# Splitting the 64-wide attention's scores into high and low fp32r parts, with its weights streamed in on every pass

## The reference

```python
def _L1_xattn_ref(x, latents, mask, ...):    # x = ctx_1024, latents = _layernorm(x_main)
    xn, ln = layernorm(x, ...), layernorm(latents, ...)
    q = ln @ Wq                                       # [256, 8 heads x 64]
    k, v = split(concatenate([xn, ln], axis=1) @ Wkv) # 512 keys: 256 of the context, 256 of the tokens
    sim = einsum('bhid,bhjd->bhij', q * scale, k) * scale
    sim = where(full_mask, sim, max_neg)              # only context keys can be masked
    attn = softmax(sim)
    out = einsum('bhij,bhjd->bhid', attn, v)
    return layernorm(out @ Wo, ...)
```

## Time and profile before

| | us |
|---|---|
| median of three runs | 5651.34 |
| profiled execution, its own time | 5660.27 |
| span of the profiled execution | 5658.5 |
| PE busy / share of the span | 4888.0 / 86% |
| DVE busy | 2758.3 / 49% |
| ACT busy | 1853.5 / 33% |
| mean granted TensorE clock, share of full speed | 0.921 |

### The profile page before, as it was taken

The page is one execution under the profiler, slowest core; times in us unless marked ns, Lnnn a source line. Parts: engine busy times, 40 slices in busy tenths (PEclk is TensorE's granted clock), DMA queues, the critical chain, the costliest instruction groups (busy, mean ns, idle before and its releaser), DMA issues.

```text
span 5658.5 us, 74258 instructions
## 1 busy us (share of the span) xinstructions
PE 4888.0 (86%) x29184; PEld 3477.8 (61%) x29184; DVE 2758.3 (49%) x7346; ACT 1853.5 (33%) x3068; POOL 95.5 (2%) x180
## 2 busy tenths in 40 slices
PE   2898878989799897998979988899888998889988
PEld 1556765567656685565855658556585565855657
DVE  3535455354553545436454454544545445454454
ACT  2422324233242333423233242332424324242242
POOL 0000000000000000000000000000000000000000
PEclk9898989999899898998989989799897998989989
DMA  6000210002000020000200002000020000200002
GB/s 273 1 1 22 88 50 1 1 22 112 26 1 1 22 112 26 1 9 21 105 26 1 15 23 97 26 1 14 31 90 26 1 22 23 90 26 1 22 23 94
DMA packets 47155, 218.95 MB, mean 39 GB/s; under 512 B 4544, under 2 KB 16832, under 8 KB 27072
## 3 DMA queue, kind: packets, MB, share of 16 engines
q1 hardware_dynamic: 46784, 213.90, 10.2%
HBM read 192.91 MB, written 20.97 MB: 38 GB/s over the span
## 4 chain that ended last, share of the span: by engine, by line
PE 70%; DVE 19%; ACT 5%; issue 3%; DMA 2%; SPq 0%; POOL 0%; DVEq 0%; ACTq 0%
PE w L418 16%; PE w L428 10%; DVE mx L1023 6%; PE o L559 6%; PE w L675 6%; PE w L517 5%; PE w L667 4%; PE w L408 4%; PE w L531 4%; PE o L552 4%; PE w L484 2%; ACT oth L786 2%; PE w L534 1%; PE w L571 1%; PE w L467 1%
## 5 line engine op out<-in xcount | busy, mean ns | idle before, releaser
L824 ACT ACTIVATE pt<-w 128x1024 f32<-128x1024 f32 x640 | 653.8, 1024 | 768.6 <-PE w L534 440.4
L1023 DVE TENSOR_REDUCE mx<-w 128x4 f32<-128x1024 f32 x512 | 593.7, 1218 | 171.9 <-PE w L467 155.1
L559 PE MATMUL o<-pt,va 128*32 128x256 f32 x4096 | 559.5, 410 | 18.7 <-ACT pt L824 18.7
L786 ACT ACTIVATE oth<-w,res 128x256 f32<-128x256 f32 x656 | 264.1, 475 | 731.0 <-PE w L667 599.8
L1259 DVE TENSOR_REDUCE mx<-w 128x2 f32<-128x1024 f32 x128 | 156.9, 1226 | 527.0 <-PE w L519 527.0
L418 PE MATMUL w<-xnT,res 128*128 128x256 f32 x1408 | 375.3, 418 | 33.8 <-ACT xnT L778 24.5
L667 PE MATMUL w<-qsp,ksp 128*128 128x256 f32 x2048 | 350.3, 289 | 0.0
L418 PEld LDWEIGHTS w<-xnT,res 128*128 128x128 f32 x1408 | 281.3, 208 | 98.8 <-issue 47.6
L559 PEld LDWEIGHTS o<-pt,va 128*32 128x32 f32 x4096 | 207.9, 114 | 194.1 <-issue 67.8
L467 PE MATMUL w<-ksp,qsp 32*128 32x256 f32 (+1 forms) x2048 | 260.9, 401 | 73.5 <-DVE mx L1023 41.5
L418 PE MATMUL w<-xnT,stream 128*128 128x256 f32 x1280 | 311.8, 391 | 0.0
(11 more groups left out here) (235 smaller groups left out, 7506.6 us busy)
## 6 DMA issues: line engine op xcount, KB each, us to landing
stream_lo<-split SPq DMA_DIRECT2D x64, 1024.0 KB, 4.8
ksp<-split SPq DMA_DIRECT2D x64, 1024.0 KB, 6.9
stream<-in_moe_dram SPq DMA_DIRECT2D x80, 384.0 KB, 3.6
va<-in_moe_dram SPq DMA_DIRECT2D x8, 1024.0 KB, 10.3
split<-ksp SPq DMA_DIRECT2D x8, 1024.0 KB, 5.6
split<-qsp SPq DMA_DIRECT2D x8, 1024.0 KB, 8.0
res<-in_resident_dram SPq DMA_DIRECT2D x1, 8157.5 KB, 22.1
cx<-in_ctx_dram SPq DMA_DIRECT2D x16, 256.0 KB, 3.6
```

Source lines behind the costliest of these rows:

```text
L559: mm = pe.matmul(o[g:g + 32, 0:T], by_heads(plan, s)[:, kt, plan.v_of(h), :], pt[:, n % EXPS, a * 512 + kt * T:a * 512 + (kt + 1) * T], st ...
L786: h = act.activation(dst[:, c, :], w[:, c * T:(c + 1) * T], func, bias=bias[:, c:c + 1], **more)
L824: act.activation(pt[:, n % EXPS, :], w[:, :], ACT.Exp, scale=scale).then_inc(S["s_P"], 1)
L1023: dve.tensor_reduce(mx[s][:, :, 2 * u:2 * u + 2].rearrange("p t a -> p a t"), w[:, :].rearrange("p (a t k) -> p a t k", a=2, t=TT), AX_X, ...
```

## The change

- The score matmuls of `l1` are done in fp32r. `k1` now has one chunk per head: 64 partitions hold the rounded keys (high), the other 64 hold what the rounding lost (low). Per head there are two matmuls instead of one fp32 one: the rounded query, laid out twice over both halves (in `qsp`), against the stacked keys, and the query's low part, with zeros in the other half, against the same keys. The product of both low parts is left out.
- Low parts of even heads lie over `xnT` and `xt`, which are idle then; those of odd heads have a buffer `qodd` of their own, zeroed once before the loop. DVE zeroes half of the shared ones in each `l1.q`.
- `l1.q` costs ACT four copies of 64 partitions and DVE two memsets and three subtractions; `l1.kc` and `l1.kl` cost ACT two copies and DVE two subtractions. A new semaphore tells DVE that ACT's copy is done, and the PSUM buffer is free only after DVE's subtraction.
- The mask's two operands become 128 rows high, `maskb` and `first_row`, with zeros below row 0.
- To make room, `l1_wkv`, `l1_wq`, `l1_wo` (4096 columns, 2 MB) and `f3_w1` (2048 columns, 1 MB) leave the resident block. In each pass the first three are loaded into `stream`, between the context and the tokens in SP's list, and `f3_w1` after the seventh `f2` expert. The first five `f1` experts wait until the `l1` weights under them have been used, in both slots.
- `ORDER` is unchanged.

```diff
-        ksp, k1 = shared("ksp", [P, 8, T], F32R, "k1", [P, 4, L1_KEYS])
+        k1, ksp = shared("k1", [P, L1_HEADS, L1_KEYS], F32R, "ksp", [P, 8, T], F32R)
+        qodd = per_slot("qodd", [P, 4, T], F32R)
...
+        def q_low(s, h):
+            return (qodd[s][:, h // 2, :] if h % 2 else q_even[s][h // 4][:, h // 2 % 2, :])
...
                 if what in ("cT", "xT"):
+                    pe.wait_ge(S["s_l1w"], 16)
...
-                        pe.matmul(w[:, tt * 512:(tt + 1) * 512], qz[s][:, u, tt * P:(tt + 1) * P],
-                                  k1[s][:, u // 2, :], start=True, stop=False)
-                        mm = pe.matmul(w[:, tt * 512:tt * 512 + T], ones_row[:, 0:P], maskb[s][:, :], start=False, stop=True)
+                        for n, q in enumerate((qsp[s][:, u, :], q_low(s, u))):
+                            pe.matmul(w[:, tt * 512:(tt + 1) * 512], q[:, tt * P:(tt + 1) * P], k1[s][:, u, :],
+                                      start=(n == 0), stop=False)
+                        mm = pe.matmul(w[:, tt * 512:tt * 512 + T], first_row[:, 0:P], maskb[s][:, :], start=False, stop=True)
...
-                        pe.matmul(o, k1[s][:, u // 2, kt * P:(kt + 1) * P], qz[s][:, u, :], start=True, stop=False)
+                        for n, q in enumerate((qsp[s][:, u, :], q_low(s, u))):
+                            pe.matmul(o, k1[s][:, u, kt * P:(kt + 1) * P], q, start=(n == 0), stop=False)
...
                     elif step == "l1.q":
                         w = full(act, step, s)
-                        for half in range(2):
-                            h = act.activation(qz[s][:, half::2, :], chunks_of(w, 4), ACT.Copy, scale=W_["half"][:, half:half + 1])
-                        h.then_inc(S["s_qz"], 1)
+                        for odd in range(2):
+                            for rows in range(2):
+                                h = act.activation(qsp[s][64 * rows:64 * rows + 64, odd::2, :],
+                                                   chunks_of(w, 4)[64 * odd:64 * odd + 64], ACT.Copy)
+                        h.then_inc(S["s_qhi"], 1)
                     elif step in ("l1.kc", "l1.kl"):
-                        evac(k1[s][:, :, o:o + T], chunks_of(full(act, step, s), 4), "s_k1")
+                        for odd in range(2):
+                            r = slice(64 * odd, 64 * odd + 64)
+                            h = act.activation(k1[s][r, odd::2, o:o + T], chunks_of(w, 4)[r], ACT.Copy)
+                        h.then_inc(S["s_k1hi"], 1)
...
+                    elif step == "l1.q":                      # DVE
+                        for part in q_even[s]:
+                            dve.memset(part[64:128].bitcast(F32), 0.0)
+                        dve.wait_ge(*after("s_qhi", step, s))
+                        for n, part in enumerate(q_even[s]):
+                            dve.tensor_tensor(part[0:64], w[0:64, 2 * n:2 * n + 2], qsp[s][0:64, 4 * n:4 * n + 4:2, :].bitcast(F32), ALU.subtract)
+                        h = dve.tensor_tensor(qodd[s][64:128], w[64:128], qsp[s][64:128, 1::2, :].bitcast(F32), ALU.subtract)
+                        h.then_inc(S["s_qz"], 1)
+                    elif step in ("l1.kc", "l1.kl"):          # DVE
+                        dve.wait_ge(*after("s_k1hi", step, s))
+                        for odd in range(2):
+                            r, other = slice(64 * odd, 64 * odd + 64), slice(64 - 64 * odd, 128 - 64 * odd)
+                            h = dve.tensor_tensor(k1[s][other, odd::2, o:o + T], w[r], k1[s][r, odd::2, o:o + T].bitcast(F32), ALU.subtract)
+                        h.then_inc(S["s_k1"], 1)
...
+                sp.dma_start(stream[:, :], resident_in[:, RESIDENT_COLS:RESIDENT_COLS + LATE_COLS]).then_inc(S["s_l1w"], 16)
                 sp.wait_ge(s_out, 16 * SLOTS)
...
+                        for name, steps in (("l1_wkv", ("l1.kc", "l1.vc", "l1.kl", "l1.vl")), ("l1_wq", ("l1.q",)), ("l1_wo", ("l1.out",))):
+                            if n * MOE1_COLS < late[name][1] and (n + 1) * MOE1_COLS > late[name][0]:
+                                for step in steps:
+                                    used(step, 0)
...
+                for e in range(MOE2 - RING2, MOE2):
+                    if e % RING2 == 0:
+                        used("f2.down", e)
+                sp.dma_start(stream[:, 0:2048], resident_in[:, RESIDENT_COLS + LATE_COLS:]).then_inc(S["s_f3w"], 16)
```

More of the change, by code:

```diff
@@ L55 @@
     ("l3_wq", 512), ("l3_wk", 512), ("l3_wv", 512), ("l3_bq", 2), ("l3_bk", 2), ("l3_bv", 256),
[1 row of a table removed]
[1 row of a table added]
 ]
+LATE = [("l1_wkv", 2048), ("l1_wq", 1024), ("l1_wo", 1024)]
+LAST = [("f3_w1", 2048)]
 RESIDENT_COLS = sum(n for _, n in RESIDENT)
+LATE_COLS = sum(n for _, n in LATE)
+RESIDENT = RESIDENT + LATE + LAST
 STAGE = [("sel8q", 256), ("sel8k", 256), ("sel16q", 256), ("sel16k", 256), ("sel1", 1024), ("f3_w2", 2048)]
@@ L238, in build @@
         at, W_ = 0, {}
-        for name, n in RESIDENT:
+        for name, n in RESIDENT[:-len(LATE + LAST)]:
             W_[name] = res[:, at:at + n]
@@ L262, in build @@
         stream_lo = over("stream_lo", [P, STREAM_COLS])
+        W_["f3_w1"] = stream[:, 0:2048]
+        late, at = {}, 0
+        for name, n in LATE:
+            W_[name] = stream[:, at:at + n]
+            late[name] = (at, at + n)
+            at += n
         pt = sb("pt", [P, EXPS, 1024])
@@ L1172, in _ @@
             dve.memset(onesf[:, :], 1.0)
-            dve.memset(ones_row[:, :], 1.0)
+            dve.memset(first_row[:, :], 0.0)
+            for s in range(SLOTS):
+                dve.memset(maskb[s][:, :], 0.0)
+                dve.memset(qodd[s][:, :, :].bitcast(F32), 0.0)
             dve.memset(mp[:, :, :], 0.0)
```

34 lines of the change are left out of this document (21 added, 13 removed), and 4 rows, old and new, of tables (RESIDENT, SIGNALS).

## The result

| | before | after |
|---|---|---|
| median, us | 5651.34 | 5613.78 (5 runs, 5613.03 to 5617.67) |
| ratio, 95% interval | | 0.9943 [0.9925, 0.9962] |
| span of the profiled execution, us | 5658.5 | 5611.2 |
| mean granted TensorE clock | 0.921 | 0.901 |
| mean length of passes 2 to 8, us | 694.9 | 690.9 |

The account below looks back on a forecast made before the run. PE was taken to bound the `l1` attention. Per pass 39.6 us removed, 22.8 plus 6 for the clock added, net 10.8; with the start 91 in eight passes, giving 5560 us, range 5465 to 5660 (forecast's own 5500 to 5620).

Parts of the forecast that it names:

- PE work removed: `l1` scores: `l1.exp` 18.2 us and `l1.max` 21.4 us less on PE, together 39.6 us a pass.
- Rival 1: Half-height copies and subtractions take half the time and the clock stays up: 13.9 us a pass more, 5449; chance 0.10.
- Start of a pass: Tokens and mask land 5.3 us later behind the 2 MB load; 1.1 us of slack, so 4.2 lost a pass.
- `l1.kc`, slot 0: Slot 1's `l0.norm` waits in DVE's queue behind the key subtractions; PE's transposes come 4.2 us later.
- `l1.kc`, slot 1: Turn, add and `l1.ln` of slot 0 wait behind DVE's subtractions; transposes of `l1.xT` start 5.0 us later.
- `l1.q`: Slot 0: slot 1's turn waits behind DVE's query subtractions; PE's transposes of its result start 6.0 us later.
- Clock: Lower granted clock behind three new holes, about 2 us each: 6 us a pass, bounds 0 and 14.
- In-stage waits: Second slot's `l1.q` and `l1.kl`, and `l1.max` meeting DVE's reductions and turns: 3.4 us a pass, between 0 and 8.
- Once: Before the first pass: smaller resident block, less DVE's memsets, saves 5 us once (0 to 8.3).
- Rival 2: Mask matmul keeps 0.31 us instead of 0.12: 12.2 us a pass, time 5657, no measurable change; chance 0.15.
- Rival 3: Clock stays low through the `l1` scores after the holes: slower, 5744 with half of them affected; chance 0.07.
- Rival 4: Freed PE time goes to waits in `l1`, 15 us a pass instead of 3.4: 5653; chance 0.08.

Follow-up runs that it names:

- fill: Changed kernel with five extra fp32 matmuls, results unused, on PE ahead of the waits of `l0.xT:0` and `f0.cT:1:1`: 5574.81 us, ratio 0.9856.
- mask_row: Changed kernel with the mask's two operands one row high again: 5695.29 us, ratio 1.0073 to the kernel before.
- before_mask: Kernel before the change with only the mask's operands made 128 rows high: 5516.12 us, ratio 0.9777.

## Why the prediction was right in direction and wrong in size

- **PE work removed, 39.6 us: right, in part by luck.** From the table of tiles it is 16 x (2 x 0.674 + 2 x 0.390 + 2 x 0.182) = 39.9. Inside it two errors cancel: the mask's part is 16.1 us, not 12.2, and the split's is 23.8, not 27.4. The fp32r matmuls of 512 columns start 0.31 and 0.24 us apart from what follows, near the value taken and far from the bound of 0.53.
- **Durations of ACT and DVE: right.** A copy of 64 partitions takes 4.11 / 4 = 1.03 us, a subtraction 1.23. Rival 1 (half height, half time) is refuted.
- **Start of a pass, 4.2 us: mis-sized.** I took tokens and mask 5.3 us late. They came 6.9 us late in the fourth pass (17.20 for 10.34), 6.0 by the median of seven. Of the 1.1 us of slack little was there: PE starts `l0.xT` 5.6 us later. It then runs at half clock, which brings 9.9, of which 7.5 are left at the end of `l0`; the sum had 6.2 with its share of the clock. Moving the load is worth 6.6 a pass.
- **`l1.kc`, slot 0, 4.2 us: right at its place, and short behind it.** The transposes of `l0.oT` stand 4.4 us later against the end of `l1.kc`, but up to the end of `l0.out` it is 6.1, since `l0.out` runs at half clock (3.78 us for 1.97). I had given this one of the four holes no share of the clock.
- **`l1.kc`, slot 1, 5.0 us**: 5.3 in the trace, for the 7.0 with its share of the clock, and mostly through another wait, 3.39 us for the PSUM buffer; the late `l1.ln` holds `l1.xT` up for 1.25. I had cost the late release of a buffer nowhere.
- **`l1.q`, 6.0 us: right**, 6.00 in the trace. With the slower steps behind it the place costs 9.0 (18.1 to 27.0), beside the 8 that the sum had for it with its share of the clock.
- **Clock, 6 us: short, inside its bounds.** From 0.921 and 0.901 the time at the low level is 0.079 x 5658 / 0.5 = 894 us before and 1111 after, 27 a pass more; in passes 2 to 8 it is 112 and 143 a pass, 32 more. At 0.24 to 0.38 us for each, as between passes of one kernel, that is an estimated 8 to 12 us; it lies partly in the terms above. `fill` shows 6 us a pass for two places alone.
- **In-stage waits, 3.4 us**: 39.9 less the 34.8 measured is 5.1.
- **Behind `l1`**: I forecast nothing, and 1.8 us a pass are lost there by the median, 2.1 by the mean. I had put the later loads of the `f1` experts and of `f3_w1` at nothing, but whether they cause it stays open.
- **Once, 5 us: right.** The first pass begins 6.0 us earlier.

By the mean the sum on the trace is 28.6 + 5.1 + 2.1 = 35.8 us added a pass for the 28.8 predicted, and 39.9 removed: a pass wins 4.1 us, not 10.8. The profiled executions fall by 47 us where the forecast had 91, the medians by 38. The step that failed is the sum of what is added, and in it the price of a hole. I priced each by its length, with a flat 2 us of clock for three of them and none for the fourth, 25.4 together, and the slow steps behind them bring it to 27.0 by the median and 28.6 by the mean. The rest is 1.7 more within the scores and about 2 behind them, which I had at nothing. No single term is far out: the forecast was a small difference of two large sums, and 7 us of error in one of them took more than half of it.

The forecast's own range was also too narrow for what it names: with the clock at 14 and the in-stage waits at 8 the sum gives 5661, with both at nothing 5485, not 5620 and 5500. Rival 2 (the mask keeps 0.31) fell with `mask_row` and `before_mask`. Rival 3 did not come: from 2376 to 2382 us, amid the scores, the granted clock reads 1.00. Rival 4 had freed time lost to waits within `l1`; much of it was lost, but ahead of the scores, not in them.
